# Perceiver layer on one core: attention halves of tile 0 moved apart, router weights combined on chip, value projection unsplit in the last two tiles, filler matmuls in tile 0's first waits

## The reference, cut to what matters

```python
x = x + _L0_xattn_ref(_layernorm(x), ctx_4096, ...)      # fake_quant(h) @ fake_quant(ctx[b])
x = x + _L0_attn_ref(_layernorm(x), wq, bq, wk, bk, wv, bv, ...)
#   q, k, v = h @ w.T + b, shape (B, S, 32 heads, 16)
#   scores = einsum('bshd,bstd->bsht', q, k) / 4;  context = einsum('bsht,bstd->bshd', softmax(scores), v)
x = x + _L0_ffn_ref(_layernorm(x), A_w, B_w, Wq_w, keys)
#   scores = (h @ Wq_w.T) @ keys.T                       # 512 -> 16 -> 64
#   gate = softmax over the 16 largest of 64
#   out = ((h @ A_w.T) * gate per expert) @ B_w.T * 2
```

## Time and profile before

| | us |
|---|---|
| median of 3 runs | 167.67 (166.19 to 168.75) |
| the profiled execution | 163.3 |
| its span, first to last instruction | 161.2 |
| TensorE matmul busy | 133.5 (83% of the span) |
| VectorE busy | 90.3 (56%) |
| ScalarE busy | 61.4 (38%) |
| GpSimd busy | 46.8 (29%) |
| DMA, 24.52 MB | saturated until about 62 us, then nearly idle |

### The profile page before, as it was taken

One profiled execution on the slowest core, in us unless ns is written; L12 is line 12 of the kernel. 1 busy time (PEld: TensorE's weight loads), 2 busy tenths in 40 slices (PEclk: granted clock), 3 DMA queues, 4 the chain that ended last, 5 costly groups with the idle time before them and its releaser, 6 DMA issues.

```text
span 161.2 us, 5802 instructions
## 1 busy us (share of the span) xinstructions
PE 133.5 (83%) x2636; PEld 79.8 (50%) x2636; DVE 90.3 (56%) x183; ACT 61.4 (38%) x73; POOL 46.8 (29%) x62
## 2 busy tenths in 40 slices
PE   0059497999982969699959999999999999879993
PEld 0023483447750643456534664765464466445772
DVE  0441871067794419537993456899144949475322
ACT  0399876851372910417691902133110231011110
POOL 3227114652146318704254094020005200001000
PEclk9999999999999586999999999999999999999999
DMA  2899999999999984000000100000010000000101
GB/s 61 335 427 400 412 396 423 398 408 422 421 358 408 361 342 187 4 0 4 4 6 6 69 0 0 4 4 4 4 65 4 0 6 4 4 4 0 65 0 65
DMA packets 7098, 24.52 MB, mean 152 GB/s; under 512 B 1185, under 2 KB 1441, under 8 KB 5154
## 3 DMA queue, kind: packets, MB, share of 16 engines
q1 hardware_dynamic: 6928, 24.16, 38.4%
q10 hardware_dynamic: 146, 0.01, 0.1%
HBM read 23.11 MB, written 1.05 MB: 150 GB/s over the span
## 4 chain that ended last, share of the span: by engine, by line
PE 64%; DMA 9%; ACT 8%; issue 8%; DVE 6%; POOL 2%; ACTq 0%; POOLq 0%; DVEq 0%
PE ps_b L983 20%; PE ps_a L983 20%; DMA raw<-in_ctx_dram 7%; PE ps_att L1053 5%; PE ps_att L1041 5%; ACT cu L413 5%; PE ps L925 3%; DMA sc_in<-in_quant_dram 3%; PE ps L1022 2%; PE ps_t L963 2%; PE ps_t L951 1%; DVE gate L734 1%; POOL cbf L324 1%; PE ps_b L1097 1%; PE ps_a L1097 1%
## 5 line engine op out<-in xcount | busy, mean ns | idle before, releaser
L324 POOL TENSOR_SCALAR cbf<-cu 128x2048 bf16<-128x2048 uint8 x14 | 26.6, 1897 | 32.9 <-ACT cu L413 31.1
L413 ACT ACTIVATE cu<-raw,sc_in,sc_recip 128x2048 uint8<-128x2048 f32 x15 | 31.1, 2089 | 6.5 <-DMA raw<-in_ctx_dram 6.4
L312 POOL TENSOR_SCALAR var_eps<-mean_var 128x1 f32<-128x1 f32 x12 | 2.7, 228 | 48.4 <-DVE mean_var L552 48.2
L1053 PE MATMUL ps_att<-vT,eT 32*32 32x17 f32 x1024 | 11.3, 183 | 6.5 <-issue 5.8
L1053 PEld LDWEIGHTS ps_att<-vT,eT 32*32 32x32 f32 x1024 | 10.1, 108 | 12.0 <-issue 9.6
L983 PE MATMUL ps_a<-wq,h2T 128*128 128x512 f32 x16 | 10.3, 803 | 0.8 <-ACT h2T L420 0.7
L1041 PE MATMUL ps_att<-kT,qT 16*32 16x32 f32 x1024 | 10.6, 193 | 0.1
L1041 PEld LDWEIGHTS ps_att<-kT,qT 16*32 16x32 f32 x1024 | 9.6, 104 | 1.1 <-issue 0.8
L983 PE MATMUL ps_a<-wk,h2T 128*128 128x512 f32 x16 | 9.0, 706 | 1.1 <-issue 1.1
L925 PEld LDWEIGHTS ps<-q1T,cbf 128*128 128x128 bf16 x256 | 7.3, 98 | 5.1 <-issue 3.2
L902 PE MATMUL ps_t<-ident_bf,q 128*128 128x128 bf16 x12 | 1.4, 248 | 9.9 <-DVE q L575 9.9
(11 more groups left out here) (127 smaller groups left out, 225.8 us busy)
## 6 DMA issues: line engine op xcount, KB each, us to landing
raw<-in_ctx_dram SPq DMA_DIRECT2D x15, 1024.0 KB, 12.1
raw<-in_ctx_dram SPq DMA_DIRECT2D x2, 512.0 KB, 12.2
wq<-in_L_attn_wq_dram SPq DMA_DIRECT2D x1, 1024.0 KB, 14.4
wk<-in_L_attn_wk_dram SPq DMA_DIRECT2D x1, 1024.0 KB, 12.8
wv<-in_L_attn_wv_dram SPq DMA_DIRECT2D x1, 1024.0 KB, 17.9
wa<-in_L_ffn_A_w_dram SPq DMA_DIRECT2D x1, 1024.0 KB, 13.6
wb<-in_L_ffn_B_w_dram SPq DMA_DIRECT2D x1, 1024.0 KB, 15.8
out_dram<-x_sb SPq DMA_DIRECT2D x3, 256.0 KB, 2.0
```

What stands on the lines that cost most here:

```text
L324: nc.gpsimd.tensor_scalar(cbf[:, n % BF_SLOTS, :, :], cu8[:, n % U8_SLOTS, :], -CENTER, 1.0, ALU.add, ALU.mult).then_inc(sem_ctx_bf_pool, 1)
L413: nc.scalar.activation(cu8[:, n % U8_SLOTS, :], raw[:, n % RAW_SLOTS, :], ACT.Identity, bias=sc_in[:, 3:4], scale=sc_recip[:, 2:3]).then_i ...
L1053: last = nc.tensor.matmul(ps_att[rows, i, 0:HD + 1], eT[rows, i, :], vT[rows, i, :], start=True, stop=True)
```

## The change

Five edits. (1) On TensorE tile 0's part 1 of the attention and tile 1's projections are regrouped: `project_q(1)` whole, context part 0, `project_k(1)` whole, context part 1, where each context half stood in the middle of or right behind q; tile 1's scores part 0 stands between v's halves. VectorE, ScalarE and GpSimd lists follow. (2) The router's weights are multiplied once: four transposes of `wr` and four matmuls with `keys` give `wr_keys` (512 x 64), so that a tile's router is four matmuls of h3T with 64 columns and no copy. The two loads move ahead of context 5 in SyncE's list. (3) In tiles 2 and 3 `project_v` is no longer split. (4) Tile 3: the bottleneck of tile 2 is cut 1 + 2 + 1 around scores part 1 and context part 0, where it was 2 + 2. (5) Two filler matmuls ahead of context 3's product and two behind it; five fillers in tile 0 become three, and three more come behind tile 1's scores.

```diff
@@ SyncE @@
             sp.dma_start(wk[:, :, :], chunked(wkT)).then_inc(sem_wk_in, 16)
+            sp.dma_start(wr[:, :, :], chunked(wrT)).then_inc(sem_router_in, 16)
+            sp.dma_start(keys[:, :], keysT).then_inc(sem_router_in, 16)
...
             for n in range(2 * BPT, 3 * BPT):
                 load_ctx(n)
-            sp.dma_start(wr[:, :, :], chunked(wrT)).then_inc(sem_router_in, 16)
-            sp.dma_start(keys[:, :], keysT).then_inc(sem_router_in, 16)
@@ ScalarE @@
-            def copy_router_q(t):
...
-                nc.scalar.copy(router_qT[:, :], ps1[0:RD, 0, RS:RS + P]).then_inc(sem_router_q_ready, 1)
+            def copy_router_rows():
+
+                act.wait_ge(sem_wr_transposed, 1)
+                nc.scalar.copy(wr_rows[:, :], ps_t1[0:RD, :]).then_inc(sem_wr_rows, 1)
+
+            def copy_router_weights():
+
+                act.wait_ge(sem_wr_keys_done, 1)
+                nc.scalar.copy(wr_keys[:, :, :], ps_b[:, 0:KC * E]).then_inc(sem_wr_keys, 1)
@@ VectorE, behind transpose_v(0) @@
+            softmax_shift(0, 1)
             dve.wait_ge(sem_x_rest_in, 16)
             norm_stats(x_sb[:, 2, :], 0, 2, sem_ln1_stats, sem_ln1_mean)
-            softmax_shift(0, 1)
+            transpose_probs(0, 1)
+            bias_q(1)
+            spread_heads(qT, q_sb, sem_q_biased, sem_qT_ready, 1)
             norm_1(2)
@@ TensorE @@
                 pe.wait_ge(sem_h2_ready, t + 1)
                 if t == 1:
-                    pe.wait_ge(sem_h2T_ready, 1)
+                    pe.wait_ge(sem_wr_rows, 1)
...
-            def router_q(t):
...
-                    last = nc.tensor.matmul(ps1[0:RD, 0, RS:RS + P], wr[:, c, :], h3T[:, c, :], start=(c == 0),
...
+            def transpose_router_weights():
+
+                pe.wait_ge(sem_router_in, 32)
+                pe.wait_ge(sem_h2T_ready, 1)
+                for c in range(KC):
+                    last = nc.tensor.transpose(ps_t1[0:RD, c * P:(c + 1) * P], wr[:, c, :], ident[:, :])
+                last.then_inc(sem_wr_transposed, 1)
+
+            def combine_router_weights():
+
+                pe.wait_ge(sem_wr_rows, 1)
+                pe.wait_ge(sem_k_biased, 1)
+                for c in range(KC):
+                    last = nc.tensor.matmul(ps_b[:, c * E:(c + 1) * E], wr_rows[:, c * P:(c + 1) * P],
+                                            keys[:, :], start=True, stop=True)
+                last.then_inc(sem_wr_keys_done, 1)
...
+                    last = nc.tensor.matmul(ps1[:, 1, RS:RS + E], h3T[:, c, :], wr_keys[:, c, :], start=(c == 0),
...
-            product(0)
+            product(0, 0, BPT - 1)
+            keep_clock_up(2, ps_t1[:, 0:P])
+            product(0, BPT - 1, BPT)
+            keep_clock_up(2, ps_t1[:, 0:P])
             transpose_y1(0)
...
             project_v(0, second)
-            keep_clock_up(5)
+            transpose_router_weights()
+            keep_clock_up(3)
+            combine_router_weights()
             transpose_h2(1)
             scores(0, 1)
-            project_q(1, first)
+            project_q(1)
             context(0, 0)
-            project_q(1, second)
+            project_k(1)
             context(0, 1)
```

More of the change, by code:

```diff
@@ L381, in _ @@
                 if u + 2 < TILES:
-                    center_ctx(BPT * (u + 2) + 1)
-                    center_ctx(BPT * (u + 2) + 2)
-                    center_ctx(BPT * (u + 2) + 3)
+                    for n in range(BPT * (u + 2), BPT * (u + 3)):
+                        center_ctx(n)
             rsqrt(2, TILES - 1, sem_ln3_mean, sem_ln3_eps, sem_ln3_rstd)
@@ new lines, in _ @@
+            bias_k(1)
+            transpose_context(0)
+            spread_heads(kT, k_sb, sem_k_biased, sem_kT_ready, 1)
+            finish_product(2)
+            norm_3(0)
+            softmax_shift(1, 0)
+            residual_1(2)
+            bias_v(1)
+            transpose_v(1)
+            transpose_probs(1, 0)
+            softmax_shift(1, 1)
+            norm_1(3)
+            choose_experts(0)
+            transpose_probs(1, 1)
+            gates(0)
+            center_q1(3)
+            row_sum_term(3)
@@ new lines, in _ @@
+            gate_z(0)
+            sum_gates(0)
+            for u in range(2, TILES):
+                residual_3(u - 2)
+                transpose_context(u - 1)
+                bias_q(u)
+                spread_heads(qT, q_sb, sem_q_biased, sem_qT_ready, u)
+                if u + 1 < TILES:
+                    finish_product(u + 1)
+                norm_3(u - 1)
+                bias_k(u)
+                spread_heads(kT, k_sb, sem_k_biased, sem_kT_ready, u)
+                bias_v(u)
+                transpose_v(u)
+                softmax_shift(u, 0)
+                if u + 1 < TILES:
+                    residual_1(u + 1)
+                choose_experts(u - 1)
+                transpose_probs(u, 0)
+                softmax_shift(u, 1)
+                gates(u - 1)
+                if u + 1 < TILES:
+                    gate_z(u - 1)
+                    transpose_probs(u, 1)
+                else:
@@ L885, in _ @@
+            residual_2(t)
+            norm_stats(x_sb[:, t, :], 2, t, sem_ln3_stats, sem_ln3_mean)
+            dve.wait_ge(sem_h3_transposed, 2 * t)
+            norm_apply(h3[:, :], x_sb[:, t, :], 2, t, sem_ln3_rstd, sem_h3_ready)
+            residual_3(t - 1)
+            choose_experts(t)
+            gates(t)
+            last_gate_z()
+            sum_gates(t)
             last_residual_3()
@@ L1007, in project_k, with project_v @@
                 project(product_bank(1, t), h2T, wk, sem_k_done)
-            def project_v(t, chunks):
+            def project_v(t, chunks=range(KC)):
                 if chunks[0] == 0:
@@ L1101, in last_output, with keep_clock_up @@
                     last.then_inc(sem_out_done, 1)
-            def keep_clock_up(count):
+            def keep_clock_up(count, dst=ps1[:, 0, 512 - P:512]):
                 for _ in range(count):
-                    nc.tensor.matmul(ps1[:, 0, 512 - P:512], ident[:, :], ident[:, :], start=True, stop=True)
+                    nc.tensor.matmul(dst, ident[:, :], ident[:, :], start=True, stop=True)
             first, second = range(0, KC // 2), range(KC // 2, KC)
-            most, rest = range(0, KC - 1), range(KC - 1, KC)
             transpose_q1(0)
             spread_biases()
-            product(0)
+            product(0, 0, BPT - 1)
+            keep_clock_up(2, ps_t1[:, 0:P])
+            product(0, BPT - 1, BPT)
+            keep_clock_up(2, ps_t1[:, 0:P])
             transpose_y1(0)
@@ new lines, in _ @@
+            transpose_q1(2)
+            product(2)
+            project_v(1, first)
+            scores(1, 0)
+            project_v(1, second)
+            transpose_y1(2)
+            scores(1, 1)
+            transpose_h3(0)
+            keep_clock_up(3)
+            router_scores(0)
+            bottleneck(0, range(KC))
+            context(1, 0)
+            transpose_zg(0)
+            output(0)
+            transpose_q1(3)
+            transpose_h2(2)
+            context(1, 1)
+            project_q(2)
@@ new lines, in _ @@
+            product(3)
+            project_k(2)
+            project_v(2)
+            transpose_h3(1)
+            scores(2, 0)
+            transpose_y1(3)
+            router_scores(1)
+            scores(2, 1)
+            bottleneck(1, range(KC))
+            context(2, 0)
+            transpose_zg(1)
+            output(1)
+            transpose_h2(3)
+            context(2, 1)
+            project_q(3)
+            project_k(3)
+            project_v(3)
+            transpose_h3(2)
+            scores(3, 0)
@@ L1167, in _ @@
+            router_scores(2)
+            bottleneck(2, range(0, 1))
+            scores(3, 1)
+            bottleneck(2, range(1, KC - 1))
+            context(3, 0)
+            bottleneck(2, range(KC - 1, KC))
+            context(3, 1)
+            transpose_zg(2)
+            output(2)
+            keep_clock_up(5)
             t = TILES - 1
             transpose_h3(t)
-            router_q(t)
-            last_z_half(0, range(0, 1))
             router_scores(t)
-            last_z_half(0, range(1, KC))
+            last_z_half(0, range(KC))
```

166 lines of the change are left out of this document (43 added, 123 removed).

## The result

| | before | changed |
|---|---|---|
| median of 20 runs each, us | 167.06 (161.09 to 170.71) | 167.93 (165.08 to 172.08) |
| the profiled execution, us | 163.3 | 167.4 |
| its span, us | 161.2 | 165.6 |
| mean granted clock | 0.979 | 0.938 |

The ratio is 1.0283, 95% interval 1.0213 to 1.0353: slower. The forecast of the direction and the range held. The predicted 171.1 us is 3.2 us above the median measured: it was 3.4 us on top of a median of three runs.

The account below looks back on a forecast made before the run. TensorE was taken to bound the kernel, with instruction supply stopping it in tiny matmuls. Terms 0 + 0.2 - 1.0 + 0 + 2.6 + 1.1 + 0.3 + 0.6 - 0.4 gave +3.4 on 167.67: 171.1 us, range 163 to 175.5.

Parts of the forecast that it names:

- portions of 256: TensorE's list comes in 256-instruction portions, each requested when the previous begins; turnaround 4.0 us idle, 6.2 to 6.7 during loads.
- the last router, -1.0: Last tile: first bottleneck piece, copy and second router matmul leave the path, saving 1.0 us (0.8 to 1.2).
- tile 2, +2.6 and +1.1: Tile 2, scores to bottleneck: instruction gaps add 2.6 us (2.0 to 3.3), the lower clock behind them 1.1 in the mean.
- the portion comes 3.2 to 3.9 us in: Tile 2: the second portion arrives this late while TensorE needs 2.6 us, giving a gap of about 0.7 to 1.3.
- tile 1, "hangs on VectorE, as before": Tile 1's end still waits for the gated z; tiles 0 and 1 sum to 0 us, from -3 to +2.
- early fillers, 0: Tile 0's start: fillers change nothing, bounds -3.3 to +0.5 us; q of tile 0 under 5 us would prove the prediction wrong.
- rival C: Early fillers bring tile 0's q to full rate, -3.3 us, two thirds given back; +2.3, 170.0 us, chance 0.06.
- tile 3, +0.3 and +0.6: Tile 3: supply gaps add 0.3 us (-0.4 to +1), lower clock for the output 0.6; three gaps sum to over 3.
- tile 0's gap of 5 us and the low clock behind it: End of tile 0's scores part 1: one 5 us gap replaces 3.10; longer gaps may cost low clock, +0.7.
- A (the clock holds): Rival: instruction supply binds but the clock does not fall; +1.0 us, 168.7 us, chance 0.22.
- B: Rival: marks do not bind in the new places, tile 2's scores run into the bottleneck gapless; -4.8, 162.9 us, chance 0.22.
- D: Rival: low clock lasts through bottleneck and output in tiles 2 and 3, gaps at upper bounds; +6.5, 174.2 us, chance 0.12.

Follow-up runs that it names:

- e1: The changed kernel without the four early filler matmuls around context 3's product in tile 0; 167.67 us, ratio 1.0314 to the kernel before.
- f1: The kernel before plus only the four early filler matmuls; 166.65 us, ratio 1.0233 to the kernel before.
- f2: The kernel before plus only the combined router weights, all orders as before; 167.06 us, ratio 1.0252 to the kernel before.
- f3: The kernel before plus the early fillers and the combined router weights, without the new orders; 166.66 us, ratio 1.025 to the kernel before.
- g2: The changed kernel with tile 1's gate first and without the early fillers and tile 1's fillers; 162.95 us against 167.65 before.
- g1: The changed kernel with tile 1's gate first and without tile 1's three fillers, a repeat of f4; 165.59 us against 167.65 before.
- h1: g2 once more; 163.53 us against 166.29 for the kernel before, ratio 0.9866.
- e4: The changed kernel with tile 1's gate ahead of the work for tile 3 on VectorE and ScalarE; 166.82 us, ratio 1.0332 to the kernel before.
- g3: g1 with tile 2's value projection split again, one of four matmuls between the scores halves; 170.55 us against 167.65 before.
- f4: The changed kernel with tile 1's gate first and without tile 1's three fillers; 164.83 us, ratio 1.0137 to the kernel before.
- e2: The changed kernel without the three filler matmuls behind tile 1's scores; 169.40 us, ratio 1.0469 to the kernel before.

## Why the prediction was right, and where it was wrong

**Right: the reading of "issue" as portions of 256.** The two large gaps stand at the records that were counted (end of scores part 1 in tile 0, end of scores part 1 in tile 2), and e1, f1, f2, f3 and g2 moved them by the instructions that they take or add. The reading held for every kernel here. The Trainium skill (Runtime: NRT & Kernel Launch, section Instruction fetch mechanics) says that such a crossing is mostly hidden. Of some 20 crossings most are, those among large matmuls; in bursts of tiny ones they are not, with 4.57, 2.20, 1.04, 0.87 and 0.63 us in the changed kernel.

**Right: the last router, -1.0.** From its first record to the gated transposes 3.74 us (157.96 less 154.22), where it was 4.67 (153.56 less 148.89): -0.9.

**Right in kind, too large in one part: tile 2, +2.6 and +1.1.** The gap at the scores' end came (2.20 for 2.6). The one of 0.7 to 1.3 us at the router did not: the router took 1.23 us where g1 and h1 show 1.00, so it was 0.2. From the scores' start to the bottleneck TensorE took 6.5 us (111.17 less 104.64), not 7.2: with v's 0.9 ahead, +2.0. The failed step is "the portion comes 3.2 to 3.9 us in": behind a stretch of large matmuls it came no later than 2.8 us after the mark. The clock's price was sized from q and k, 1.1; the bottleneck, met by the lower clock over most of its length, cost 2.4. Sum 4.4 for 3.7.

**Wrong: tile 1, "hangs on VectorE, as before".** I took 0 and -0.4 and looked only at what TensorE's list drops. TensorE came 2.2 us early to the gate, and the new order of VectorE had put the centring of tile 3's activations (0.69 + 0.08 + 0.27 us and 0.45 of waiting for ScalarE) ahead of it. "Moves VectorE steps but drops none" was true and no reason for a zero: the order decides. e4 shows it for 1.2 of the 1.7 us. The norm of 1.73 us (the median of this line's seven is 0.55) stands beside 3.76 us of GpSimd's centring; e4 has it too (1.75), so it is not what e4 won. But all ten profiles with the new order of VectorE have it at 1.73 to 1.75 us and the four with the old one at 0.53, so it belongs to the new order as well; no run takes it away alone.

**Wrong: early fillers, 0, "as the row is".** q of tile 0 took 3.70 us, and the prediction had named that itself as a sign of being wrong (under 5 us). So this term has failed: rival C described what came, the gain and its return to the waits behind. But the cause that C and I both named is not shown either. Of the nine profiles with early fillers eight have q at 3.70 and one, g3, at 6.20; of the five without them two (g2 and h1) have 3.70, the others 5.09, 6.58 and 6.62, and g2, h1, e1 and before have the same list on TensorE up to there. The fillers make the full clock likelier at most. g1 against g2 puts what they cost in the end at about 2.6 us, from six executions each that overlap.

**Wrong in part: tile 3, +0.3 and +0.6.** The gaps sum to 1.67 us (0.63 and 1.04), and some 0.2 inside the scores (1.48 for 1.29), not over 3, and the output kept the full clock. From scores part 1 to the last router 15.5 us (154.22 less 138.72) stand against 16.1 (148.89 less 132.82).

**Right: tile 0's gap of 5 us and the low clock behind it.** 4.57 us, and q of tile 1 took 5.68. The third gap was 0.87, not 1.4.

By the terms, in the two profiled executions: -1.5 by the start of tile 0's scores (38.25 for 39.78; 0 was taken), a further 0.7 up to the gate, +1.7 for the gate's wait and +1.7 for the clock behind it, +4.4 in tile 2 (3.7 taken), and -0.6 and -0.9 at the end (tile 3 and the last router). With +0.3 between tile 2's bottleneck and tile 3's scores part 1 that is the 4.4 us. That the sum of +3.4 came near is in part luck: a gain at the start and a loss in tile 1, neither of them counted, nearly cancel. Lucky too is the base, since of the 3.4 us the medians over all executions show 0.9. One more reading was off without a price: the two router loads went 24 us earlier in SyncE's queue (11.68 for 35.74), not 12.

**The rivals.** A (the clock holds) is refuted by the 6.12 us bottleneck. B is refuted by its own test: the scores of tile 2 end in a gap. D was not reached.

**What stays open.** Why a portion comes 3.3 to 4.0 us after the mark in some places and within 2.8 in others. In h1 the mark at the head of tile 2's context is followed by the next 256 instructions on, at the gated transposes, 2.3 us later at most, with hardly a stop. In all the short cases the earlier mark lies within a dozen records behind a run of large matmuls, which would fit an issuing side that is ahead of execution there; no run separates it. How much of g2's gain is marks and how much is the clock is open too, since the clock mostly falls behind stops and no run moves one without the other. It does not need one: in tile 2 of f2 the output took 5.40 us with no stop on issue near it, only 0.73 us of waiting for VectorE.

## What to carry to other kernels

When an engine stands still on "issue" in bursts of tiny instructions, count instructions between the stops; if the count is constant, the place of each stop can be worked out for any edit, and enough large matmuls should lie between one mark and the next to cover the time of a portion (here 3.3 to 4.0 us with idle DMA engines, 6.2 to 6.7 while the loads run). Instructions added far upstream, fillers too, then have a price that does not stand where they are: here leaving out sixteen of them went with about 2.6 us less in one version (g2 against g1) and with nothing in another (e1). After a reordering look at each engine that is waited for: what stands ahead of the awaited step in its own list is the price, not what the list holds in sum.

## What was not expected of the hardware

The granted clock fell behind stops of 1.8 to 4.9 us beside tiny matmuls, and a whole projection right behind took 5.3 to 6.5 us for 3.70. Behind shorter ones it went both ways: behind a stop of 1.31 us at the end of tile 3's attention the output took 3.70 us in h1 and 5.40 in f4, at 1.04 in the changed kernel 3.70 and in e1 and e2 5.22 and 5.32. Two executions of one list up to q of tile 0 gave 3.70 and 6.62 us. The wide scatter of every kernel's times goes with it: the same program took 161.09 to 170.71 us, and among the eleven executions of it timed with g1 the fastest (161.26) has a mean granted clock of 0.968 and the slowest (171.36) 0.926. Whether the clock makes all of it is not shown. While the loads ran, a portion took 6.2 to 6.7 us again (50.84 to 57.13 in h1).
